# Sparse product of an expert layer: both rank fills of a chunk in one group, a block of the second product spread out, and VectorE's rounds without a loop

## What is computed

```
q = h @ Wq;  sim = q . keys                     # 2 x 4 heads x 64 keys
sx, sy = top 8 of each half;  all = sx + sy     # 64 candidates per head
scores = top 8 of all;  idx = their expert numbers (of 1024)
w = silu(h . down_embed[idx]) * softmax(scores)
experts = sum of w * up_embed[idx]
mlp = (silu(h @ Wg + bg) * (h @ Wu + bu)) @ Wd + bd
x = x + mlp + experts
```

## Time and profile before

| | |
|---|---|
| median of 3 runs | 2409.92 us (2403.93 to 2412.46) |
| the profiled execution | 2408.92 us |
| its span, first to last instruction | 2407.2 us |
| busy, TensorE / VectorE / ScalarE | 92% / 79% / 47% |
| the two expert layers | about 477 to 1235 us and 1648 to 2404 us |
| mean granted TensorE clock | 0.987 |

### The profile page before, as it was taken

One profiled execution on the slowest core, in us unless ns is written; L12 is line 12 of the kernel. 1 busy time (PEld: TensorE's weight loads), 2 busy tenths in 40 slices (PEclk: granted clock), 3 DMA queues, 4 the chain that ended last, 5 costly groups with the idle time before them and its releaser, 6 DMA issues. The chain is left out here.

```text
span 2407.2 us, 37844 instructions
## 1 busy us (share of the span) xinstructions
PE 2224.7 (92%) x12582; PEld 1548.4 (64%) x12582; DVE 1902.4 (79%) x5516; ACT 1127.6 (47%) x1542; POOL 80.9 (3%) x135
## 2 busy tenths in 40 slices
PE   5999999899999999999979999988999999999998
PEld 4777777676576676676734455446576576675674
DVE  5768686689889898998965566556888889898997
ACT  1445454453543544434426666663543544444533
POOL 3200000000000000000000000000000000000000
PEclk9999999999999999999989999999999999999999
DMA  7000000000000000000000000000000000000000
GB/s 210 1 1 0 0 0 1 1 1 1 0 0 0 0 0 0 0 0 0 1 1 1 1 1 0 1 1 1 1 9 9 0 9 9 0 9 9 0 10 9
DMA packets 20761, 18.10 MB, mean 8 GB/s; under 512 B 6555, under 2 KB 19871, under 8 KB 20648
## 3 DMA queue, kind: packets, MB, share of 16 engines
q1 hardware_dynamic: 16106, 14.04, 1.9%
q10 hardware_dynamic: 4542, 2.78, 0.4%
HBM read 12.60 MB, written 4.19 MB: 7 GB/s over the span
## 5 line engine op out<-in xcount | busy, mean ns | idle before, releaser
L1380 ACT ACTIVATE f_E<-f_two 128x1024 f32<-128x1024 f32 x256 | 248.2, 1021 | 324.8 <-PE f_two L1265 324.8
L1111 DVE SCALAR_TENSOR_TENSOR f_E<-f_two,f_E 128x1024 f32<-128x1024 f32 x256 | 311.2, 1221 | 91.1 <-ACT f_E L1380 84.7
L1255 PE MATMUL f_acc<-ue,f_mid 128*128 128x256 f32 x1024 | 251.9, 392 | 6.2 <-DVE f_mid L1096 6.2
L1255 PEld LDWEIGHTS f_acc<-ue,f_mid 128*128 128x128 f32 x1024 | 191.0, 193 | 47.4 <-issue 15.4
L1163 PE MATMUL f_two<-f_hT,wg 128*128 128x512 f32 x768 | 210.3, 409 | 0.0
L1350 ACT ACTIVATE f_gate<-f_two,bg 128x512 f32<-128x512 f32 x128 | 88.1, 688 | 257.6 <-PE f_two L1163 257.3
L1163 PE MATMUL f_two<-f_hT,wu 128*128 128x512 f32 x768 | 199.9, 395 | 0.0
L1835 ACT ACTIVATE b_U<-b_two 128x768 f32<-128x768 f32 (+1 forms) x192 | 158.8, 882 | 65.5 <-PE b_two L1700 64.8
L1163 PE MATMUL f_two<-f_hT,deT 128*128 128x512 f32 x768 | 184.3, 395 | 0.0
L1591 DVE TENSOR_TENSOR b_U<-b_U,tri 128x512 f32<-128x512 f32 x128 | 85.4, 689 | 116.3 <-ACT b_U L1835 116.3
L1163 PEld LDWEIGHTS f_two<-f_hT,wu 128*128 128x128 f32 x768 | 144.2, 188 | 35.0
(11 more groups left out here) (262 smaller groups left out, 3950.7 us busy)
## 6 DMA issues: line engine op xcount, KB each, us to landing
x<-in_L_attn_a_x SPq DMA_DIRECT2D x8, 512.0 KB, 7.5
out_x<-x SPq DMA_DIRECT2D x8, 512.0 KB, 2.9
de_rows<-in_L_ffn_down_embed ACTq DMA_DIRECT2D x1, 1024.0 KB, 6.0
wd<-in_L_ffn_Wd SPq DMA_DIRECT2D x1, 1024.0 KB, 10.1
ue<-in_L_ffn_up_embed SPq DMA_DIRECT2D x16, 64.0 KB, 5.2
whole_g<-in_L_ffn_Wg SPq DMA_DIRECT2D x1, 1024.0 KB, 5.4
whole_u<-in_L_ffn_Wu SPq DMA_DIRECT2D x1, 1024.0 KB, 8.7
ffq<-in_L_ffn_Wq ACTq DMA_DIRECT2D x4, 128.0 KB, 8.9
```

The source lines that it names most:

```text
L1111: dve.scalar_tensor_tensor(out=two_heads, in0=wide(turns, ("R", u))[:], scalar=PICKED_ABOVE, in1=two_heads, op0=ALU.is_gt, op1=ALU.mult).t ...
L1255: mm = pe.matmul(acc[:, j * C:(j + 1) * C], mixed[c % 2][:, j * P:(j + 1) * P], w.ue[:, c, :], start=False, stop=True, skip_group_check=True)
L1380: act.activation(E[:, c % 2, 2 * p:2 * p + 2].rearrange("p h t -> p (h t)"), wide(turns, ("S", u))[:], ACT.Exp).then_inc(S.act_read, 1)
```

## The change

It does six things.

- The two rank fills of a chunk are issued one behind the other in one group (from chunk 2 on), as the two score fills already were. Both claims now stand ahead of the first matmul, for score and rank fills alike. The tiles that stood between the rank fills go ahead of the group or behind it; in chunks 0 and 1 one gap between R(2c) and R(2c+1) stays.
- `AHEAD` is 2. `mlp_out(2)` is no longer one block at the end of the dense part: one of its tiles goes ahead of the turning of "z", and three go into chunks 0 and 1. `mlp_out(0)` and `mlp_out(1)` stand behind `gates(4)` and `gates(6)` instead of `gates(3)` and `gates(4)`.
- DVE copies all of "d", and ACT copies "s" in two halves, the first as soon as the first quarter is turned. PE waits for the first half by a semaphore of its own.
- `gated(0)` is put behind `highest(1)` and `half_code(0)`.
- The fill "o" (the share of experts beyond the table) goes behind R(15), not ahead of it.
- DVE's rounds 0 to 6 are written out, so that the loop and its registers are gone.

```diff
-        AHEAD = 3
-        LATE_TILES = [(0, 1, 2), (1, 2, 2), (1, 2, 0), (1, 2, 0), (0, 0, 0), (1, 2, 0), (1, 2, 0), (0, 0, 0)]
+        AHEAD = 2
+        LATE_TILES = [(1, 1), (2, 3), (2, 0), (2, 1), (2, 1), (2, 1), (2, 1), (2, 0)]
...
-        sparse.insert(len(sparse) - 1, ("o", 0))
+        sparse.append(("o", 0))
...
-                    gated(0)
                     for t in range(1, TJ):
                         highest(t)
                         half_code(t - 1)
+                        if t == 1:
+                            gated(0)
...
-                    dve.tensor_scalar(digitsT[:, 2:4, :], codes[:, 2:4, :], 1.0 / 2048, None, ALU.mult
-                                      ).then_inc(S.dve_read, 1)
+                    dve.tensor_scalar(digitsT[:], codes, 1.0 / 2048, None, ALU.mult).then_inc(S.dve_read, 1)
...
-                a_round(0, steady, first=True, last=False)
-                with dve.Fori(0, (ROUNDS - 2) // 2) as n:
-                    for m in range(2):
-                        a_round(n * 2 + m + 1, steady, first=False, last=False)
+                for i in range(ROUNDS - 1):
+                    a_round(i, steady, first=(i == 0), last=False)
...
-                        if f in (3, 4):
-                            mlp_out(f - 3)
-                    mlp_out(AHEAD - 1)
+                        if f in (4, 6):
+                            mlp_out(f // 2 - AHEAD)
...
+                        if q == 2:
+                            late_out(1)
...
+                        if q == 0:
+                            mm.then_inc(S.half_turned, 1)
...
+                    def fill(names, stationary, moving):
+                        outs = [claim(i, turns, name) for name in names]
+                        for out, (_, u) in zip(outs, names):
+                            lq, hh = u // 4, u // 2 % 2
+                            for h in (u % 2 * 2, u % 2 * 2 + 1):
+                                rows = slice(32 * h, 32 * h + 32)
+                                mm = pe.matmul(out[:, (h % 2) * T:(h % 2 + 1) * T],
+                                               stationary[rows, hh].rearrange("r a l -> r (a l)"), moving[rows, lq, :],
+                                               start=True, stop=True)
+                            mm.then_inc(S.filled, 1)
+
+                    pe.wait_ge(S.opening_scores, i + 1 + START)
+                    pe.wait_ge(*turns.dve_has_read(i, ("d", 0)))
...
+                        fill([("S", 2 * c), ("S", 2 * c + 1)], w.sel, scoreT)
+                        if c < 2:
+                            fill([("R", 2 * c)], w.selb, digitsT)
+                            late_out(LATE_TILES[c][0])
+                            fill([("R", 2 * c + 1)], w.selb, digitsT)
+                        else:
+                            late_out(LATE_TILES[c][0])
+                            fill([("R", 2 * c), ("R", 2 * c + 1)], w.selb, digitsT)
...
-                        fill(("R", 2 * c + 1), w.selb, digitsT)
-                        late_out(LATE_TILES[c][2])
+                        late_out(LATE_TILES[c][1])
...
-                    act.activation(digitsT[:, 0:2, :], codes[:, 0:2, :], ACT.Copy, scale=1.0 / 2048
-                                   ).then_inc(S.act_read, 1)
+                    opening = wide(turns, ("s", 0))
+                    act.wait_ge(S.half_turned, i + 1 + START)
+                    act.activation(scoreT[:, 0, :], opening[:, 0:T], ACT.Copy).then_inc(S.opening_scores, 1)
                     act.wait_ge(*turns.filled(i, ("s", 0)))
-                    act.activation(scoreT[:, 0:2, :].rearrange("p q t -> p (q t)"), wide(turns, ("s", 0))[:], ACT.Copy
-                                   ).then_inc(S.act_read, 1)
+                    act.activation(scoreT[:, 1, :], opening[:, T:2 * T], ACT.Copy).then_inc(S.act_read, 1)
```

More of the change, by code:

```diff
@@ L78, in __init__ @@
             "dve_read sim_half sim_first rank_step below_ready expo_ready total_ready ln_ready digits_ready "
-            "lo_scores shifted heads_added mix_step mix_ready mix_used mid_used x_added "
+            "lo_scores shifted heads_added mix_step mix_ready mix_used mid_used x_added half_turned opening_scores "
         ).split()]
@@ L84, in __init__ @@
          self.ln_ready, self.digits_ready, self.lo_scores, self.shifted, self.heads_added, self.mix_step,
-         self.mix_ready, self.mix_used, self.mid_used, self.x_added) = self.all
+         self.mix_ready, self.mix_used, self.mid_used, self.x_added, self.half_turned,
+         self.opening_scores) = self.all
 class AttnSignals:
@@ L865, in experts_ffn @@
         RANK_STEPS = 44
-        readers = {"x": "both", "m": "act", "r": "act", "g": "both", "d": "both", "s": "act", "z": "dve",
+        readers = {"x": "both", "m": "act", "r": "act", "g": "both", "d": "dve", "s": "act", "z": "dve",
                    "o": "dve", "S": "act", "R": "dve"}
@@ L1098, in add_heads @@
                     def add_heads(c):
-                        dve.wait_ge(*turns.dve_has_read(i, ("R", 2 * c + 1)))
+                        dve.wait_ge(*turns.dve_has_read(i, ("R", 2 * c + 1) if c < FC - 1 else ("o", 0)))
                         if c == 1:
@@ L1112, in a_round @@
                                                  in1=two_heads, op0=ALU.is_gt, op1=ALU.mult).then_inc(S.dve_read, 1)
-                        if u == UNITS - 2:
+                        if u == UNITS - 1:
                             last_rows = E[96:P, c % 2, 0]
                             dve.wait_ge(*turns.filled(i, ("o", 0)))
-                            dve.wait_ge(*turns.dve_has_read(i, ("R", u)))
+                            dve.wait_ge(*turns.dve_has_read(i, ("R", u - 1)))
                             dve.tensor_tensor(last_rows, wide(turns, ("o", 0))[96:P, 0:T], last_rows, ALU.add
@@ L1257, in experts @@
                         mm.then_inc(S.mix_used, 1)
-                    def fill(name, stationary, moving):
-                        u = name[1]
-                        lq, hh = u // 4, u // 2 % 2
-                        out = claim(i, turns, name)
-                        for h in (u % 2 * 2, u % 2 * 2 + 1):
-                            rows = slice(32 * h, 32 * h + 32)
-                            mm = pe.matmul(out[:, (h % 2) * T:(h % 2 + 1) * T],
-                                           stationary[rows, hh].rearrange("r a l -> r (a l)"), moving[rows, lq, :],
-                                           start=True, stop=True)
-                        mm.then_inc(S.filled, 1)
-                    pe.wait_ge(*turns.act_has_read(i, ("s", 0)))
-                    pe.wait_ge(*turns.act_has_read(i, ("d", 0)))
+                    def fill(names, stationary, moving):
[10 more added lines that the diff above has]
+                    pe.wait_ge(*turns.dve_has_read(i, ("d", 0)))
                     for c in range(FC):
@@ L1274, in a_round @@
                             pe.wait_ge(*turns.dve_has_read(i, ("z", 0)))
-                        for p in range(2):
-                            fill(("S", 2 * c + p), w.sel, scoreT)
-                        late_out(LATE_TILES[c][0])
-                        fill(("R", 2 * c), w.selb, digitsT)
-                        late_out(LATE_TILES[c][1])
+                        fill([("S", 2 * c), ("S", 2 * c + 1)], w.sel, scoreT)
[6 more added lines that the diff above has]
+                            fill([("R", 2 * c), ("R", 2 * c + 1)], w.selb, digitsT)
                         if c == FC - 1:
@@ L1367, in a_round @@
                     act.activation(idle[:, 1:2], w.eps[:, 0:1], ACT.Exp)
-                    act.wait_ge(*turns.filled(i, ("d", 0)))
-                    codes = wide(turns, ("d", 0))[:].bitcast(I16).rearrange("p (q t) -> p q t", t=T)
-                    act.activation(digitsT[:, 0:2, :], codes[:, 0:2, :], ACT.Copy, scale=1.0 / 2048
-                                   ).then_inc(S.act_read, 1)
+                    opening = wide(turns, ("s", 0))
+                    act.wait_ge(S.half_turned, i + 1 + START)
+                    act.activation(scoreT[:, 0, :], opening[:, 0:T], ACT.Copy).then_inc(S.opening_scores, 1)
                     act.wait_ge(*turns.filled(i, ("s", 0)))
-                    act.activation(scoreT[:, 0:2, :].rearrange("p q t -> p (q t)"), wide(turns, ("s", 0))[:], ACT.Copy
-                                   ).then_inc(S.act_read, 1)
+                    act.activation(scoreT[:, 1, :], opening[:, T:2 * T], ACT.Copy).then_inc(S.act_read, 1)
                     for u in range(UNITS):
```

## The result

The changed kernel takes 2369.78 us (median of 4 runs, 2365.48 to 2372.08), the kernel before 2409.19 us on the same chip (2403.93 to 2412.46). The ratio is 0.9834, with a 95% interval of [0.982, 0.9848]: 39.4 us less, where 36 were forecast (2373, range 2361 to 2396). Beside the first batch one execution of the kernel before took 10620 us, and its ratios leave it out.

What follows compares the result with a forecast made beforehand. PE's own program, gaps included, was taken as the bound, with a few waits for ACT and DVE. Opening -1.05 and sparse part -1.3 gave 2.35 us per round; with the last rounds, 36.5 off, 2373 us, range 2361 to 2396.

Steps and rivals of the forecast that it cites:

- more than forecast: Rival, chance 0.07: filling the 0.99 wait may end TensorE's clock fall in chunk 4, 1 to 2 us per call; 2362.
- The opening, -1.05: Before S(0): ACT's half copies of "s" start earlier, so S(0) starts 1.05 us sooner per round, bounds 0.7 and 1.2.
- Rank fills in one group, 0.42 in place of 0.64: Chunks 2 to 7: four heads side by side take 0.42 us, not 0.64, saving 1.3 us per round.
- no more than two heads overlap: Rival, chance 0.15: rank fills gain nothing beyond two heads; 0.9 us per round less gain, 2388.
- Tiles +1.3: Sparse part: three tiles of the third block come in from the dense part, costing 1.3 us per round.
- blocks -0.8: Sparse part: 16 separate blocks of tiles between fills instead of 20, at 0.20 us each, save 0.8 per round.
- rank groups -1.3: Sparse part, chunks 2 to 7: rank fills issued in one group save 6 x 0.22 = 1.3 us per round.
- waits -0.5: Sparse part: PE's waits fall from 3.4 to 2.9 us, 0.5 less per round.
- The loop's edge: DVE's loop restart, 2.43 us, six times: hidden before; with gated(0) moved, keeping it would cost PE up to 1.8 each.
- without it 0.4 would be lost: Dense part on DVE: moving gated(0) later readies digits before PE wants them; saves nothing, but avoids losing 0.4 us.
- Reading PSUM as the bound: Rival, chance 0.15: DVE's PSUM reading keeps chunks at 5.3 us, leaving only the opening's gain of 17; 2392.
- Rounds written out starving VectorE: Rival, chance 0.06: fetching DVE's unlooped instructions stalls it 2.43 us each; one stall per round gives 2410, two 2444.

Runs made afterwards that it cites:

- the first batch: Four runs, each undoing one part of the changed kernel: rank claims, rank-fill adjacency, opening or the place of gated(0); 2364.43, 2382.76, 2380.85 and 2367.83 us.
- the best version: Changed kernel with an own claim ahead of every fill and one tile moved from chunk 6 to chunk 7, ahead of "o"; 2351.06 us, ratio 0.9754.

## Why the prediction was right

**The whole.** 36.5 forecast, 38.9 in the profiled executions (39.2 between their spans). My 2.35 a round was 2.29 from round 0 to round 0, 14 x 2.29 = 32.1 against 32.9. The last rounds gave 1.8 and 1.3, 3.1 against 3.6. The rest I had not booked under the forecast: in the kernel before, rounds at a granted clock below 1.00 cost 1.7 in the first call and 0.9 in the second, and looped rounds 0.14 each, 0.8 in a call. The changed kernel loses 0.0 and 0.2 in all. The clock's part is what I gave only to the rival "more than forecast" (chance 0.07), as 1 to 2 us per call with the wait ahead of R(9) filled, and it came: the wait is gone and no full round has a lower clock. As said above, the place of the fall speaks for that cause, and no run tests it by itself.

**The opening, -1.05.** Measured 1.13. The half copies run at 522.87 and 523.34, and take 0.58 and 0.59 where I took 0.6; they end at 523.93 with 523.8 forecast. The follow-on was at the lower end of my 0.05 to 0.33. In a round it is worth 0.84 (taken out) or 1.27 (alone, with fills that claim one by one). What I missed: in this kernel S(0) waits for the second half and not for the first, because the two score fills claim together; the half copies could have given 0.3 more, and did with own claims. Of the 1.13, ACT's earlier end is 0.85 (26.26 to 25.41 after the bias matmuls), and the follow-on, 0.05 in place of 0.33, is 0.28. The run with the opening as before keeps the 0.05, so taking the opening out shows 0.84 only. The 0.85 comes from taking "d" off ACT and not from the halves: one copy of 1.01 from 522.87 on would end at 523.88, and the second half ends at 523.93. No run moves "d" and leaves the copy of "s" whole.

**Rank fills in one group, 0.42 in place of 0.64.** The mechanism was right and the size too careful: four heads take 0.32 on four row groups, as two do. That was my lower bound; the 0.05 for each further head isn't there. The rival that no more than two heads overlap has fallen.

**Tiles +1.3, blocks -0.8, rank groups -1.3, waits -0.5.** The sum, 1.3, came out at 1.17, but two terms don't stand by themselves. With three tiles fewer in the sparse part nothing changed, so +1.3 is not a cost that the path sees. And putting back one tile between the rank fills, which undoes 0.20 + 0.32 in each of six chunks, costs 1.09 a round, not 3.1. PE's busy time in the sparse part fell by 0.29 (47.00 to 46.71) and its gaps by 0.88, where I had 0.8 and 0.5. The step that failed is that PE's program adds up: up to the first `experts` the chain over ACT and DVE sets the time, and tiles there fill waits and cost nothing. That the sum still came within 0.13 is in part luck: a cost that was not there made up for savings that did not arrive whole.

**The loop's edge "would cost PE up to 1.8 each if it stayed".** It costs 0.0 to 0.5 in the changed kernel, and there are four such stops in an execution and not six: only where the loop starts again, not where it is entered or left. I set the whole of the lost cover against PE, and left out that PE's wait for ACT ahead of S(0) swallows what comes before it.

**`gated(0)`, "without it 0.4 would be lost".** Nothing is lost, for the same reason: the 0.49 that PE waits for `digits` comes off a later wait, and S(0) stays at 25.46. The times themselves were right: `digits` is ready 0.27 ahead of PE, 0.3 forecast.

**Reading PSUM as the bound.** DVE has no gap in chunk 3: its compares start 539.45 - 534.65 = 4.80 apart, PE's chunk takes 5.02. The Trainium skill ("TensorEngine Tiling (Array Packing)", PSUM Bottleneck) says that after row tiling has sped up TensorE the copying out of PSUM may be what limits. By this trace it was near and did not decide: the sparse part got 1.17 shorter with DVE busy 44.47 of 49.23, and by another 0.75 (49.23 to 48.48, DVE busy 44.49) in the best version.

**Rounds written out starving VectorE.** No round of the changed kernel shows it: its wait for gate 0 ends with ACT's gate after 0.67, and seven rounds take 7 x 91.79.

## What to carry over

Two parts of six made the undisturbed rounds shorter: pieces that use a quarter of TensorE's rows each, issued next to each other, and a copy taken off the engine that holds up the next stage. Cutting the other copy in half helps only if the waiting work is also claimed in halves: a wait stated for a pair holds the first until the second is free. Stating all of them one by one was worth 0.71 us in each full round here, 15 us by the medians, of which 0.3 a round is the half copy's. Before filling or moving work, ask whether the next wait along would swallow it; work put into a wait that nobody else ends (the tile ahead of "o") is pure gain, and work taken away where another engine's chain sets the time is worth nothing (the third block).

## What the runs showed of the hardware

- Four bf16 matmuls of 32 rows and 512 columns on four row groups pass in 0.32 us from start to start, as two do.
- How long after its release a waiting matmul starts differs by place: S(0) follows the copy by 0.05 us in the changed kernel (523.93 to 523.98), by 0.33 in the one before (524.61 to 524.94), and by 0.23 with S(0) claimed alone (521.57 to 521.80). The trace shows PE's sequencer steps (register work and a semaphore wait) between the two: in the kernel before they run from 524.65 to 524.88, behind the release, in the changed kernel from 523.48 to 523.71, ahead of it. With S(0) alone one wait is left behind it (521.60 to 521.75). The run with the opening as before has only the claims ahead of S(0), with ACT's copy in the last of them, and S(0) follows that by 0.05 too (524.25 to 524.30). So it looks as if a release that comes early in the list of waits costs the steps behind it; no run changes only their order.
- Where its loop starts again VectorE stood for 2.43 us, and for 2.42 to 2.71 in the run with the loop put back, as idle time that ends in "issue"; rounds written out show none. On TensorE's side it was worth 0.0 to 0.7.
- Full rounds with a granted clock of 0.98 are 0.9 to 1.5 us longer than those at 1.00, with 1.5 to 1.8 more of PE's busy time. In all 16 of them the clock falls right behind the two waits of chunk 4; kernels with that wait ahead of R(9) filled have none. (The last rounds of a call, with other waits, fall to 0.98 in the changed kernel too.)
